# A four-stage residual kernel on one Trainium2 core: VectorE's side work split around x1, and the hand-over from the first phase to attention reordered

## The reference, cut to what matters

```python
x = x + (einsum('bsi,bio->bso', x, W[id]) + b[id][:, None, :])          # layer 0: one of 16 experts
x = x + (einsum('btd,od->bto', x, W) + delta(x, A[ad], Bm[ad], s[ad]))  # layer 1: shared W, rank-16 adapters
q, k, v = x @ Wq.T, x @ Wk.T, x @ Wv.T                                  # layer 2: 8 query heads, 4 K/V heads of 64
q, k = rope(rms(q)), rope(rms(k))
k_blocks, v_blocks = k_blocks.at[blk, :, off].set(k), v_blocks.at[blk, :, off].set(v)
# blk comes from the batch's table of 257 blocks of 16 tokens: a batch can read rows that another batch wrote
p = softmax(where(allowed, q @ k_all.T / 16, -inf))                     # window of 256 keys back from each token
x = x + (p @ v_all) @ Wo.T
x = x + (einsum('bct,bcd->bdt', x, w[subject]) + bias[subject])         # layer 3: mixes tokens
```

## Time and profile before

| | |
|---|---|
| runs before | 926.55, 925.12, 926.73 us; median 926.55 |
| profiled execution, its own time | 925.46 us |
| its span, first to last instruction | 923.6 us, 1.86 us less than its own time |
| granted TensorE clock, mean | 0.993 of 2.4 GHz |
| busy share of the span | TensorE 97%, VectorE 70%, GpSimd 57%, ScalarE 48% |
| first phase | up to about 481 us |
| change of phase, last projection to first scores | 481 to 497 us |
| second phase | 497 to 924 us |

### The profile page before, as it was taken

One profiled execution on the slowest core, in us unless ns is written; L12 is line 12 of the kernel. 1 busy time (PEld: TensorE's weight loads), 2 busy tenths in 40 slices (PEclk: granted clock), 3 DMA queues, 4 the chain that ended last, 5 costly groups with the idle time before them and its releaser, 6 DMA issues.

```text
span 923.6 us, 23544 instructions
## 1 busy us (share of the span) xinstructions
PE 891.7 (97%) x6499; PEld 656.4 (71%) x6499; DVE 648.3 (70%) x1858; ACT 443.9 (48%) x1191; POOL 530.4 (57%) x499
## 2 busy tenths in 40 slices
PE   6899999999999999999997999999999999999997
PEld 4467677676666767666676778787787878778785
DVE  4655455787877854458565787788877888778884
ACT  2433243333333334333323666666666666666662
POOL 2156645656565567865567656665666565665530
PEclk9999999999999999999997999999999999999999
DMA  9999988887878878788546666666666676666741
GB/s 313 343 343 357 336 300 273 270 272 254 296 253 288 260 262 292 277 279 270 186 139 183 184 207 204 186 198 203 197 215 183 203 234 198 208 185 206 230 131 48
DMA packets 100417, 218.55 MB, mean 237 GB/s; under 512 B 30187, under 2 KB 36168, under 8 KB 92178
## 3 DMA queue, kind: packets, MB, share of 16 engines
q1 hardware_dynamic: 66290, 145.27, 47.6%
q0 software_dynamic: 25088, 57.74, 21.6%
q10 hardware_dynamic: 8992, 15.00, 4.4%
HBM read 210.39 MB, written 33.86 MB: 264 GB/s over the span
## 4 chain that ended last, share of the span: by engine, by line
PE 79%; DVE 8%; DMA 5%; issue 2%; ACT 2%; ACTq 2%; SPq 1%; POOL 1%; DVEq 0%; POOLq 0%
PE banks L698 14%; PE banks L854 10%; PE banks L611 9%; PE banks L806 9%; PE banks L842 7%; PE banks L829 6%; PE banks L679 6%; PE banks L783 4%; DMA pair_b<-in_lb 3%; PE banks L890 3%; DVE later L1176 3%; PE banks L847 3%; PE banks L664 2%; PE banks L784 2%; PE banks L822 1%
## 5 line engine op out<-in xcount | busy, mean ns | idle before, releaser
L570 POOL DMA_INDIRECT ring<-new_rows,idx x128 | 129.6, 1013 | 82.6 <-PE banks L806 45.6
L1060 ACT ACTIVATE big<-big,neg_max 128x320 f32<-128x320 f32 x256 | 141.5, 555 | 3.0 <-DVE neg_max L1429 2.7
L1429 DVE CUSTOM_DVE_ANT_0 big<-banks,mask 128x320 f32<-128x320 f32 x256 | 114.6, 485 | 25.6 <-PE banks L806 24.5
L611 PE MATMUL banks<-ring 128*64 128x512 f32 x512 | 117.2, 599 | 3.8 <-DMA ring<-in_w 3.8
L1050 ACT ACTIVATE kt<-banks 128x384 f32<-128x384 f32 x128 | 62.0, 484 | 95.7 <-PE banks L784 92.9
L498 POOL TENSOR_TENSOR rms<-ss,neg_half 128x12 f32<-128x12 f32 x30 | 68.6, 2285 | 64.4 <-DVE ss L1368 64.4
L806 PE MATMUL banks<-kt,q_in 64*128 64x128 f32 (+2 forms) x768 | 88.6, 364 | 1.3 <-ACT kt L1050 1.3
L559 POOL DMA_INDIRECT ring<-new_rows,idx x64 | 61.9, 967 | 46.8 <-PE banks L829 42.5
L1466 DVE TENSOR_SCALAR big<-big,recip 128x320 f32<-128x320 f32 x256 | 85.4, 396 | 2.3
L496 POOL TENSOR_TENSOR ring<-ring 128x512 f32<-128x512 f32 x30 | 38.8, 1293 | 83.0 <-DVE ring L1247 83.0
L806 PEld LDWEIGHTS banks<-kt,q_in 64*128 64x128 f32 x768 | 74.4, 189 | 14.4 <-issue 8.6
(11 more groups left out here) (173 smaller groups left out, 2010.5 us busy)
## 6 DMA issues: line engine op xcount, KB each, us to landing
ring<-in_w SPq DMA_DIRECT2D x62, 1024.0 KB, 7.9
ring<-in_xt SPq DMA_DIRECT2D x32, 256.0 KB, 2.6
x_in<-in_x SPq DMA_DIRECT2D x32, 256.0 KB, 5.7
bias_in<-in_b SPq DMA_DIRECT2D x64, 128.0 KB, 7.8
x_dram<-x SPq DMA_DIRECT2D x32, 256.0 KB, 8.7
q_dram<-q_t ACTq DMA_DIRECT2D x32, 256.0 KB, 6.4
new_rows<-kv_out SPq DMA_DIRECT2D x32, 256.0 KB, 6.1
q_in<-q_dram SPq DMA_DIRECT2D x32, 256.0 KB, 2.7
```

Source lines behind the costliest of these rows:

```text
L570: pool.indirect_dma_start(out=kv[:, s, c, :], out_offset=None, in_=new_rows, in_offset=bass.IndirectOffsetOnAxis(ap=idx[:, b, 1 + c:2 + c] ...
L611: last = nc.tensor.matmul(ps_l0[T * h:T * h + T, :], xt[:, s, c, T * h:T * h + T], w0[:, 2 * s + h, c * D:(c + 1) * D], start=(c == 0), st ...
L1060: nc.scalar.activation(prob[:, s % 2, PLACE[g] * NK:(PLACE[g] + 1) * NK], sm[:, s % 2, g, :], ACT.Exp, bias=neg_max[:, s % 2, g:g + 1], sc ...
L1429: V.tensor_tensor_reduce(sm[:, s % 2, g, :], ps_s[g], mask[:, s % 2, k0:k0 + NK], 1.0, 3.0e38, ALU.add, ALU.min, accum_out=neg_max[:, s % ...
```

## The change

The change has four parts.

*Side work.* VectorE's side work of each step is cut in two. The first half (two of the four merges, with `count_later` where it is due; the first shift of a step's; all of the table of rows) stands before `add_x1`, behind `split_down`; the other half stands where the whole stood. The second buffer of the shifts, `rows[1]`, becomes a view of `same`, which is free by then. The transposes of the rows and the taking of the indices move from step 31 to step 30 (INDEX_STEP).

*Order of the last projections.* The last step is written out by hand. Behind it TensorE projects K/V of pairs 29, 30 and 31 first, and the queries of 29 to 31 (all but a third of pair 29's) last, into banks of their own (`q_bank`, `kv_bank`); x2 of pair 30 gets its own buffers `held_hi`, `held_lo`. The new K/V rows of pair 31 are made in `last_kv`, a part of the staging area.

*Three pairs' queries.* The rotations of pair 29 go from POOL to VectorE, like those of 30 and 31. On POOL the order is: power for K of 29, two old gathers, power for K of 30, two old gathers, power for K of 31, power for Q of 29, the new gathers of batches 0, 1 and 2 with the powers for Q of 30 and 31 behind those of batches 1 and 2. The queries of 30 and 31 are finished inside the second phase: product on VectorE at the end of steps 0 and 1, transposes on TensorE at the end of steps 1 and 2, copies and stores on ScalarE there. At the end of step 2 TensorE waits for that last copy (`qt_ready` at 32), since the bank is used again. There are 26 `keep_warm` transposes in place of 74.

*Masks.* The constant part of the mask is loaded once, early, and copied four times by ScalarE (two instructions) instead of four loads by SP; the first mask is made before `wo_lo` is split.

The diff is cut to what sets the orders; `turn` is `last_squares`, `rotate_parts` and `last_sum` in a row.

```diff
--- before.py
+++ after.py
+INDEX_STEP = NP - 2
+LATE = NP - 3
...
-        rows = [sb(f"rows{i}", [P, ROWLEN]) for i in range(2)]
+        rows = [sb("rows0", [P, ROWLEN]), same[:, :, :].rearrange("p m r -> p (m r)")[:, 0:ROWLEN]]
...
+            held_hi, held_lo = (sb(n, [P, DC, P], F32R, first) for n in ("held_hi", "held_lo"))
...
+        def q_bank(k):
+            return (ps_kv, ps_l1)[k - LATE - 1] if late(k, LATE + 1) else ps_q
+        def kv_bank(k):
+            return ps_t1 if late(k, NP - 1) else ps_kv
...
+            last_pow(NP - 3, 1)
             make_table(NP - 1, 1, NP // 2)
-            last_pow(NP - 2, 8, 12, 1)
             pool.wait_ge(idx_ready, 1)
+            pool.wait_ge(l0_done, NP - 1)
+            for b in range(KV_EARLY - 2):
+                gather_old(b)
+            last_pow(NP - 2, 1)
             pool.wait_ge(l0_done, NP)
-            for b in range(KV_EARLY - 1):
+            for b in range(KV_EARLY - 2, KV_EARLY):
                 gather_old(b)
-            last_pow(NP - 1, 8, 12, 3)
-            gather_old(KV_EARLY - 1)
-            last_pow(NP - 2, 0, 8, 2)
-            pool.wait_ge(h_done, NP)
-            pool.wait_ge(kv_done, NP)
-            pool.wait_ge(q_done, NP)
-            nc.gpsimd.memset(bd[:, :, :], 0.0).then_inc(pool_set, 1)
-            last_pow(NP - 1, 0, 8, 4)
+            last_pow(NP - 1, 1)
+            pool.wait_ge(st_kv[0], NP // 2 * 16)
+            last_pow(NP - 3, 0)
...
-            for s in range(2):
-                pool.wait_ge(st_kv[s], NP // 2 * 16)
+            pool.wait_ge(st_kv[1], NP // 2 * 16)
             gather_new(0)
+            pool.wait_ge(q_done, NP)
+            nc.gpsimd.memset(bd[:, :, :], 0.0).then_inc(pool_set, 1)
             for b in range(1, NB):
                 gather_new(b)
+                if b <= 2:
+                    last_pow(NP - 3 + b, 0)
...
-            loop(pe, phase_one, 2, 6, NP, NP - 2)
+            loop(pe, phase_one, 2, 6, NP - 1, NP - 2)
+            adapt_down(NP - 2, 0)
+            experts(NP - 1, NP // 2 - 1, 1)
+            adapt_up(NP - 2, 0)
+            project_kv(NP - 3)
+            transpose_x1(NP - 1, 1)
+            transpose_x2(NP - 2, 0)
+            transpose_queries(NP - 4, 0)
+            project_q(NP - 3, (0,))
             adapt_down(NP - 1, 1)
-            project_kv(NP - 2)
+            project_hidden(NP - 1)
             adapt_up(NP - 1, 1)
-            project_q(NP - 2, (0, 1))
+            project_kv(NP - 2, (0, 1))
             transpose_x2(NP - 1, 1)
-            project_q(NP - 2, (2,))
+            project_kv(NP - 2, (2,))
             project_kv(NP - 1)
+            project_q(NP - 3, (1, 2))
+            project_q(NP - 2)
+            project_q(NP - 1)
             transpose_queries(NP - 3, 1)
-            project_q(NP - 1)
             pe.wait_ge(x1_ready, NP)
-            keep_warm(WARM_Q)
-            transpose_queries(NP - 2, 0)
-            keep_warm(WARM_Q)
-            transpose_queries(NP - 1, 1)
-            pe.wait_ge(idx_ready, 1)
-            pe.wait_ge(x2_ready, NP)
+            keep_warm(WARM_KEYS)
             pe.wait_ge(abk_ready, NP)
-            pe.wait_ge(abq_ready, NP)
-            pe.wait_ge(sqq_ready, NP)
             pe.wait_ge(sqv_ready, NP)
-            pe.wait_ge(qt_ready, NP)
+            pe.wait_ge(x2lo_ready, NP)
+            pe.wait_ge(qt_ready, LATE)
...
+                if isinstance(b, int) and 1 <= b <= 2:
+                    transpose_queries(LATE + b, (LATE + b) % 2)
+                if isinstance(b, int) and b == 2:
+                    pe.wait_ge(qt_ready, NP)
...
             round_down(NP - 1)
+            round_x2(NP - 1)
             square_k(NP - 2).then_inc(sqk_last, 1)
-            copy_values(0, NP // 2 - 1)
-            round_x2(NP - 1, x1t_hi)
+            copy_values(NP - 2, 0, NP // 2 - 1)
+            square_k(NP - 1).then_inc(sqk_last, 1)
+            copy_values(NP - 1, 1, NP // 2 - 1)
+            square_q(NP - 3)
             square_q(NP - 2)
-            copy_queries(NP - 3, 1, NP // 2 - 2)
-            store_queries(NP - 3, 1)
-            square_k(NP - 1).then_inc(sqk_last, 1)
-            copy_values(1, NP // 2 - 1)
-            square_q(NP - 1)
-            copy_queries(NP - 2, 0, NP // 2 - 1)
-            store_queries(NP - 2, 0)
             act.wait_ge(ld_wo, 16)
             act.wait_ge(h_done, NP)
             nc.scalar.activation(wo_hi[:, :, :], wo_stage, ACT.Copy).then_inc(wo_hi_ready, 1)
-            copy_queries(NP - 1, 1, NP // 2 - 1)
-            store_queries(NP - 1, 1)
+            square_q(NP - 1)
+            act.wait_ge(ld_mask, 16)
+            act.wait_ge(q_done, NP)
+            for k0 in (0, NK):
+                last = nc.scalar.activation(mask[:, :, k0:k0 + T], own_mask.unsqueeze(1).to_broadcast([P, 2, T]), ACT.Copy)
+            last.then_inc(mask_set, 1)
+            copy_queries(NP - 3, 1, NP // 2 - 2)
+            store_queries(NP - 3, 1)
...
+                if isinstance(b, int) and 1 <= b <= 2:
+                    copy_queries(LATE + b, (LATE + b) % 2, NP // 2 - 1)
+                    store_queries(LATE + b, (LATE + b) % 2)
...
-            SIDE = {2: take_tables, ROW_STEP: make_rows, NP - 1: take_indices}
+            SIDE = {2: take_tables, ROW_STEP: make_rows}
+            SIDE_MORE = {}
             for part in range(3):
-                SIDE[ROW_STEP + 1 + part] = lambda part=part: shift_rows(part)
+                SIDE[ROW_STEP + 1 + part] = lambda part=part: shift_rows(part, 0, 1)
+                SIDE_MORE[ROW_STEP + 1 + part] = lambda part=part: shift_rows(part, 1, 3)
             for m in range(3):
                 for part in range(MERGE_PARTS):
-                    SIDE[PREP_STEP + MERGE_PARTS * m + part] = lambda m=m, part=part: merge_runs(m, part)
+                    k = PREP_STEP + MERGE_PARTS * m + part
+                    SIDE[k] = lambda m=m, part=part: merge_runs(m, 2 * part)
+                    SIDE_MORE[k] = lambda m=m, part=part: merge_runs(m, 2 * part + 1)
...
                     split_down(k - 1)
+                if isinstance(k, int) and k in SIDE:
+                    SIDE[k]()
                 if isinstance(k, int) and k == 0:
                     dve.wait_ge(w_hi_ready, 1)
                     V.tensor_tensor(w1_lo[:, :, :], w1_stage, w1_hi[:, :, :].bitcast(F32), ALU.subtract).then_inc(w1_lo_ready, 1)
                 if on(k, 1, NP):
                     add_x2(k - 1, j - 1 + s, r)
                     split_adapters(k, s)
-                if isinstance(k, int) and k in SIDE:
-                    SIDE[k]()
+                if isinstance(k, int) and k in SIDE_MORE:
+                    SIDE_MORE[k]()
...
-            loop(dve, phase_one, 2, 6, NP, PREP_STEP)
+            loop(dve, phase_one, 2, 6, NP - 1, PREP_STEP)
+            split_down(NP - 2)
+            add_x1(NP - 1, 1)
+            add_x2(NP - 2, NP // 2 - 1, 0)
+            split_adapters(NP - 1, 1)
+            split_x1(NP - 1)
+            last_squares(NP - 3, 1)
+            split_x2(NP - 2)
+            rotate_parts(NP - 3, 1, 1)
             split_down(NP - 1)
+            last_sum(NP - 3, 1)
+            last_product(NP - 3, 1)
             add_x2(NP - 1, NP // 2 - 1, 1)
-            last_squares(NP - 2, 1)
-            rotate_parts(NP - 2, 0, 1)
-            split_x2(NP - 1, x1t_hi, x1t_lo)
+            split_x2(NP - 1)
+            turn(NP - 2, 1)
+            last_product(NP - 2, 1)
+            turn(NP - 1, 1)
+            last_product(NP - 1, 1)
+            turn(NP - 3, 0)
+            last_squares(NP - 2, 0)
+            last_product(NP - 3, 0)
             rotate_parts(NP - 2, 0, 0)
-            last_sum(NP - 2, 1)
-            last_product(NP - 2, 1, 1)
-            last_squares(NP - 2, 0)
-            last_squares(NP - 1, 1)
-            rotate_parts(NP - 1, 1, 1)
-            last_sum(NP - 1, 1)
-            last_product(NP - 1, 1, 2)
-            last_squares(NP - 1, 0)
             last_sum(NP - 2, 0)
-            last_product(NP - 2, 0, 3)
-            rotate_parts(NP - 1, 1, 0)
-            last_sum(NP - 1, 0)
-            last_product(NP - 1, 0, 4)
+            turn(NP - 1, 0)
...
+                if isinstance(b, int) and b <= 1:
+                    last_product(LATE + 1 + b, 0)
```

236 lines of the change are left out of this document (152 added, 84 removed).

## The result

The changed kernel takes 919.85 us (median of 4 runs, 918.63 to 921.55) beside 925.88 for the kernel before in the same series: ratio 0.9936, 95% interval 0.9916 to 0.9956, so 4.1 to 7.8 us less. 916.3 was forecast, a gain of 10.2, with a range of 911.5 to 921.5. It is faster, by some 6 us, and inside the range; of the four terms only one has its forecast size. The profiled execution is the slowest of the four, 921.55.

| stretch | before | after | difference | forecast |
|---|---|---|---|---|
| start to step 10 | 150.68 | 153.79 | +3.1 | 0 |
| steps 10 to 21 | 175.19 | 168.38 | -6.8 | A: -8.0, with steps 28, 29 |
| steps 22 to 27 | 84.13 | 84.63 | +0.5 | 0 |
| steps 28 and 29 | 29.45 | 28.14 | -1.3 | (A) |
| step 30 | 14.58 | 18.63 | +4.05 | B: +1.8 |

The account below looks back on a forecast made before the run. TensorE was taken as the bound, with time to win only in its waits or unneeded products. Terms -8.0 + 1.8 - 5.9 + 1.9 = -10.2 us, from 926.55 to a median of 916.3, range 911.5 to 921.5.

Parts of the forecast that it names:

- A: Steps with side work: half of it ahead of x1 removes TensorE's waits for `x1t_lo`; -8.0 us (-4.0 to -8.4).
- B: Step 30: the rows' transposes, moved there, make TensorE wait 2.4 us in the open; +1.8 us (-0.6 to +3.0).
- Rival 3: Second phase: the granted clock stays down after waits, making the kernel slower, up to +20 us, 936; chance 0.05.
- C: Change of phase: last K/V projected first, so the first gathered keys come earlier; -5.9 us (-7.0 to -3.5).
- D: Start of second phase: finishing two pairs' queries there adds a VectorE product, transposes and a copy wait; +1.9 us (0.5 to 5).
- 1: Merge steps: POOL's powers hold up the first halves, A shrinks to -4.0, time 920.3; chance 0.12.
- 2: Start of second phase: POOL's powers delay gathers of batches 2 and 3, D grows by 4, time 920.3; chance 0.12.
- 4: Steps with side work: TensorE didn't wait for the side work, so A is 0 and the time 924.3; chance 0.06.

Follow-up runs that it names:

- c_pow_first: The changed kernel with pair 31's key power on POOL ahead of the old gathers of batches 2 and 3; 917.60 us, ratio 0.9885.
- c_masks_loaded: The changed kernel with its masks' own part loaded again by four DMAs beside the first gathers, in place of ScalarE's copies; 919.36 us, ratio 0.9913.
- b_rows_before_x1: The changed kernel with all of step 30's shifts ahead of x1; 917.84 us, ratio 0.9906.
- a_side_halves: The kernel before with only the side work cut in two, one half ahead of x1, rows and indices left in step 31; 916.68 us, ratio 0.9892.
- d_queries_halves: The changed kernel with the last two pairs' queries finished in steps 3 to 6, one power for both, transposes two chunks at a time; 916.22 us, ratio 0.9876.

## Why the prediction was right, and where it was not

- **A, right.** -8.0 forecast, -8.1 in the changed kernel (-6.8 and -1.3), or -7.6 with step 27, and -8.3 alone. The halves that stand in the 2.31 us of idle time behind `split_down` run undisturbed: the two merges of step 13 take 0.70 each, the first of them inside POOL's power. What the term left out is the table of rows, all of which stands ahead of x1 in step 27 now: it ends at 398.40, x1 follows, and that step is 0.5 longer here. In the other kernels with the table there it is 0 to 1.7 longer; at 1.6, in c_pow_first, TensorE waits 1.25 for x1, and the table's last copy takes 1.25 in place of 0.72.
- **B, mis-sized.** The wait was to be 2.4 and is 2.38. "so it waits 2.4 us in the open" stopped there: the clock fell behind it, the products there cost 1.6 more, and the 0.45 of the transposes stands in this step too. That gives +4.05 in place of +1.8, outside the bounds of -0.6 to +3.0. In the two executions in which the clock didn't fall it is +2.5 and +2.6, inside them. So the step that failed is that the wait was priced at its length alone, with nothing for the clock. Rival 3 had the clock as a matter of the second phase alone.
- **C, too small.** Five thirds earlier came as forecast (4.9 with the rows). The chain behind it is 13.03 in place of 15.8: K rows 0.6 sooner, store 0.4, and from the gather to the keys 5.67 in place of 7.43. The step that failed is "the copied masks move no chain": four loads beside the gathers cost them 1.2, by c_masks_loaded. The copies may hold nothing up, but the loads that they replace had done so. The lengths 7.43 and 3.8 had been taken over from the trace of before as if they were constants. What the rest of 0.5 is was not tried; POOL's third gather goes out 2.66 behind the first, where it took 2.87.
- **D, mis-sized.** The 1.9 of products, transposes and the copy's wait are there: 1.76 in steps 1 and 2 without the powers, 1.5 of it in step 2. The prediction says of the powers "I cost them at nothing; without that cover, 2". In the profiled execution they cost 2.55 in these steps, in four of the six others at most 0.5, so "nothing" is near for most executions, and the +3.7 of the table is the upper end. The step that failed in all of them is that D ended with step 2: the 1.85 of the slower rhythm was in no term.
- **The rivals.** 1 was a real mechanism at another place: POOL's powers hold no first half (0.70 inside a power), its products and sums of two inputs do, as b_rows_before_x1 shows, 1.22 for 0.49. The Trainium skill (SBUF — State Buffer, Who interferes with whom) has VectorE's operations with two SBUF inputs and POOL's reads exclude each other; the trace agrees beside the products and disagrees beside the powers. 2 happened in part, with 2.55 of its 4 in the profiled execution and less in the others. 3 did not happen: the clock was 0.50 from 487.7 to 490.2 and near 505 to 508, and came back both times. 4 is refuted by a_side_halves.
- **The total.** The range held since the errors had both signs, B and D 5.9 dearer, C 3.1 better, so that the time fell into it is in part luck. The forecast of 916.3 lies 3.5 below the measured median. How far it is off is known to some 3 us only: d_same_loops, which differs from the change in nothing but SyncE's wait and where two loops begin, came out 9.5 us below the kernel before in its series (0.9905) where the change came out 6.0 below.

## What to carry to other kernels

A wait that is moved into the open on TensorE is to be priced at its length and at the clock that it may cost behind it: here the step became 4.0 to 4.5 us longer in five of seven executions and 2.5 in two. One trace of each kernel would have missed that, so compare a stretch over all kernels that leave it alone. Before work is put into an engine's idle time, look at which of its neighbour's instructions run there, not only at how long the gap is. When a hand-over between phases is reordered, take the duration of each landing as a thing that depends on what else is in flight, and look for small loads that can be done earlier.

## What was not expected of the hardware

- TensorE's clock fell after it stood still for 2.4 us behind a stretch without a pause: granted 1.00 during the wait, 0.85 from 445 to 447, 0.50 from 447 to 449, 1.00 again from 449.9. It did so after waits of 2.38, 2.51, 2.53, 2.75 and 2.79 us, and did not after waits of 2.47 and 2.55 in the same place. With 19 transposes that nobody reads in that wait it stayed at 1.00, in the one execution that was traced.
- A copy of 128x64 from SBUF to SBUF, 0.20 us by itself, took 1.17 on VectorE beside POOL's sum of 128x512; inside POOL's power a subtraction of 128x323 took 0.50, as by itself.
- POOL's power costs 1.01 to 1.16 us for 128x4, 1.64 to 2.03 for 128x8, 2.28 for 128x12, and 2.94 for 128x16 in one instruction (d_queries_halves), so one of 16 columns is cheaper than two of 8.
- The second phase keeps one of two paces, 25.72 or 25.84 us for four batches, for some 350 us behind a difference in its first steps; the 0.1 lies at VectorE's first maximum of every fourth batch, and why is open.
